# A four-layer graph network: block products with combined operands in layers 1 to 3, residual in HBM, projections by tile

## The reference, cut to what matters

```python
# N = 2708 nodes, 512 features, adj dense fp32 (2708 x 2708), all layers use the same adj
h = relu(layernorm(x)); x = x + relu(D(adj + I)D h @ W0)       # layer 0
h = relu(layernorm(x)); x = x + (D' adj D' h) @ W1.T + b1      # layer 1
h = relu(layernorm(x)); x = x + relu(D(adj + I)D h @ W2)       # layer 2
h = relu(layernorm(x))                                         # layer 3
x_b = adj @ (h @ Wg) + bg
e = where(adj != 0, exp(-leaky_relu(s_left[:, None] + s_right[None, :])), 0)
x_a = (e / (e.sum(1) + 1e-5)) @ (h @ Wsa)
x = x + sigmoid(gate_a * x_a + gate_b * x_b)
```

## Time and profile before

| | us |
|---|---|
| median of 3 runs | 1829.09 (1829.09 to 1830.65) |
| profiled execution | 1828.71 |
| its span, first to last instruction | 1826.9 |
| TensorE matmul busy | 1774.1 (97%) |
| VectorE busy | 900.4 (49%) |
| ScalarE busy | 693.5 (38%) |
| GpSimd busy | 273.5 (15%) |
| all DMA | 268.78 MB, mean 147 GB/s |

### The profile page before, as it was taken

How to read it: one execution, slowest core, us unless ns; L and a number is a source line. 1 busy time by engine, 2 the same in 40 slices (tenths; PEclk the granted TensorE clock), 3 DMA queues, 4 the chain that set the end, 5 groups by cost and what they waited for, 6 DMA issues and landing times.

```text
span 1826.9 us, 23918 instructions
## 1 busy us (share of the span) xinstructions
PE 1774.1 (97%) x9324; PEld 886.7 (49%) x9324; DVE 900.4 (49%) x1835; ACT 693.5 (38%) x1174; POOL 273.5 (15%) x222
## 2 busy tenths in 40 slices
PE   3999999999999999999999999999999999999996
PEld 1444446544444475444445654444466444444453
DVE  5776656656354445302032312544411577877765
ACT  5674444445333333101022212111000467768654
POOL 0001021112000000000000000311100355545431
PEclk9999999999999999999999999999999999999999
DMA  9974543575755568222431463332323333434422
GB/s 393 362 279 142 167 141 100 187 241 189 225 180 147 178 181 265 92 82 82 124 104 48 118 214 129 102 98 88 103 89 102 104 108 95 123 106 118 122 60 95
DMA packets 167425, 268.78 MB, mean 147 GB/s; under 512 B 17464, under 2 KB 78624, under 8 KB 164092
## 3 DMA queue, kind: packets, MB, share of 16 engines
q1 hardware_dynamic: 167312, 267.25, 46.4%
HBM read 208.79 MB, written 58.40 MB: 146 GB/s over the span
## 4 chain that ended last, share of the span: by engine, by line
PE 92%; ACT 3%; DVE 3%; DMA 2%; issue 0%; SPq 0%; POOL 0%; DVEq 0%; ACTq 0%
PE ps L872 25%; PE ps L873 25%; PE ps L874 25%; PE ps L824 16%; PE ps L866 1%; DMA T<-in_adj 1%; ACT T L1324 1%; DMA RG<-in_adjT 1%; DVE RG L1105 1%; ACT Q L1341 0%; ACT RG L1393 0%; PE ps L920 0%; DVE HB L1074 0%; PE ps L931 0%; ACT stage L1511 0%
## 5 line engine op out<-in xcount | busy, mean ns | idle before, releaser
L872 PE MATMUL ps<-RG,HB 128*128 128x512 f16 (+3 forms) x2368 | 836.6, 354 | 9.4 <-DVE RG L1129 3.3
L873 PE MATMUL ps<-RG,HB 128*128 128x512 f16 (+3 forms) x2368 | 836.2, 354 | 0.0
L874 PE MATMUL ps<-RG,HB 128*128 128x512 f16 (+3 forms) x2368 | 836.1, 354 | 0.0
L872 PEld LDWEIGHTS ps<-RG,HB 128*128 128x128 f16 x2368 | 232.0, 98 | 234.5 <-issue 7.5
L874 PEld LDWEIGHTS ps<-RG,HB 128*128 128x128 f16 x2368 | 231.9, 98 | 222.7 <-issue 1.9
L873 PEld LDWEIGHTS ps<-RG,HB 128*128 128x128 f16 x2368 | 231.9, 98 | 219.5 <-issue 1.9
L824 PE MATMUL ps<-W,OT 128*128 128x512 f16 (+1 forms) x1320 | 290.3, 379 | 3.5 <-DVE OT L1297 3.5
L1135 DVE SCALAR_TENSOR_TENSOR OT<-ps,OT 128x512 f16<-128x512 f32 (+2 forms) x96 | 53.5, 619 | 355.2 <-ACT OT L1441 355.2
L824 PEld LDWEIGHTS ps<-W,OT 128*128 128x128 f16 (+1 forms) x1320 | 128.2, 98 | 160.4 <-issue 4.4
L1581 POOL TENSOR_TENSOR T<-T 128x512 f32<-128x512 f32 (+2 forms) x126 | 172.9, 1372 | 180.9 <-DVE T L1119 180.3
L1105 DVE SCALAR_TENSOR_TENSOR RG<-RG,cS 128x512 f16<-128x512 f32 (+2 forms) x174 | 123.0, 720 | 136.0 <-ACT RG L1393 135.7
(11 more groups left out here) (187 smaller groups left out, 1103.6 us busy)
## 6 DMA issues: line engine op xcount, KB each, us to landing
RG<-in_adjT SPq DMA_DIRECT2D x225, 256.0 KB, 3.0
RG<-Ad SPq DMA_DIRECT2D x152, 256.0 KB, 2.6
Ad<-RG SPq DMA_DIRECT2D x84, 256.0 KB, 3.3
T<-in_adj SPq DMA_DIRECT2D x14, 1354.0 KB, 8.3
...
```

Source lines behind the costliest of these rows:

```text
L872: eng.matmul(o, h[0], hi, start=j == 0, stop=False)
L873: eng.matmul(o, h[0], lo, start=False, stop=False)
L874: last = eng.matmul(o, h[1], hi, start=False, stop=False)
```

## The change

In layers 1 to 3 the chunk's columns are cut in two halves and the features in two halves of 256. With row tiles j and j+1 as a pair, the chunk's sum over the pair is a 2x2 by 2x2 block product. It is computed with seven block products in place of eight, of combinations `T1..T4` of the adjacency blocks and `S1..S4` of the h blocks (the Strassen-Winograd form). Each of the seven products sums up in a bank of its own over ten pairs; tiles 20 and 21 are added directly as plain blocks. A matmul has half the chunk's width, 256, 128 or 202 columns. After the last pair and tile the seven sums are combined to the four output blocks (`gather`, `evacuate`); seven of eight banks are in use and the next chunk takes them over in the order of `SUMS`, the eighth (`x`) is for projections.

The combinations of the adjacency are made by GpSimd in fp32 (`sums`), then split. In layer 1 a unit (one pair, seven blocks, hi and lo) is kept in HBM, and layers 2 and 3 load units; in layer 2 the units on the diagonal are made again from raw tiles. The h combinations are made by GpSimd too (`h_sums`); there are seven slots in HB in place of four. SBUF for this comes from the residual: `xs` is gone, tiles are loaded (`x_load`) and kept (`x_keep`) in HBM through six buffers around each use. Projections are put tile by tile into the next chunk (`spaced`), for one bank. Weights for layers 1 to 3 are all split in layer 0 and loaded back.

```diff
+T2, A11, T4, A21, A22, T1, T3 = range(7)
+FIRST = ((H12, A21, "b"), (S4, A22, "d"), (S1, T1, "f"), (S3, T3, "g"))
+SECOND = ((S2, T2, "c"), (H11, A11, "a"), (H22, T4, "e"))
+SUMS = {GW: dict(a=3, b=4, c=2, d=5, e=0, f=6, g=7, x=1)}
+for _g in range(GW + 1, GE):
+    _o = SUMS[_g - 1]
+    SUMS[_g] = dict(b=_o["x"], d=_o["a"], f=_o["c"], g=_o["g"], c=_o["b"], a=_o["e"], e=_o["f"], x=_o["d"])
...
+def fly(g, j):
+    return g < 12 or g < 18 and (on_diagonal(g, j) or j < 20 and on_diagonal(g, j ^ 1)) or g >= GE
...
+    def spaced(u, g):
+        p, now = CHUNKS[g][0], g + 1
+        lead, gap = (8, 4) if now % 6 == 4 else (9, 4.5) if now % 6 in (0, 5) else (9, 9)
+        for i, t in enumerate(tiles(g)):
+            v = later(u, lead + gap * i)
+            plan(v, "project", g, t, SUMS[now]["x"])
+            if p < 3:
+                plan(max(u + 1, later(u, gap * i)), "x_load", "post", p, t)
+            post(max(v + 1, later(v, 1.5)), p, t)
...
     tensor, "agg" of layers 1 to 3
+                    if j < 20:
+                        for slot, k, to in FIRST if j % 2 == 0 else SECOND:
+                            pe.wait_ge(*h_ready(l, slot, J))
+                            if J == 0:
+                                opened(bank[to])
+                            hi, lo = operand(g, j, k)
+                            for a in range(2):
+                                o = ps[bank[to]][:, 256 * a:256 * a + n]
+                                h = [HB[:, slot, J, i, a * P:a * P + P] for i in range(2)]
+                                eng.matmul(o, h[0], hi, start=J == 0 and a == 0, stop=False)
+                                eng.matmul(o, h[0], lo, start=False, stop=False)
+                                last = eng.matmul(o, h[1], hi, start=False, stop=to in "acg" and J == 9 and a == 1)
+                    for to, o_h, o_a in (("b", 0, 0), ("d", D, n), ("e", 256, 0), ("f", 256, n)):   # tiles 20, 21
...
     gpsimd
+                elif kind == "sums":
+                    eng.tensor_tensor(unit[:, T1:T3 + 1, :], unit[:, T4:A22 + 1:2, :], unit[:, A11:T4 + 1, :],
+                                      ALU.subtract).then_inc(s_tsum, 1)
+                    pool.wait_ge(s_tsum, 3 * n - 2)
+                    eng.tensor_tensor(part[T2], part[A22], part[T1], ALU.subtract).then_inc(s_tsum, 1)
+                    pool.wait_ge(s_tsum, 3 * n - 1)
+                    eng.tensor_tensor(part[T4], part[A21], part[T2], ALU.subtract).then_inc(s_tsum, 1)
...
     scalar, vector: "gather" after tile 19, "evacuate" after tile 21
+                    eng.mul(block_of(0)[:, :, 0:half(g)], bank_halves(g, "a"), 2.0 ** -14).then_inc(s_ca, 1)
+                    eng.scalar_tensor_tensor(block_of(1)[:, :, 0:half(g)], bank_halves(g, "c"), 2.0 ** -14,
+                                             block_of(0)[:, :, 0:half(g)], ALU.mult, ALU.add).then_inc(s_cv, 1)
+                    eng.scalar_tensor_tensor(block_of(2)[:, :, 0:half(g)], bank_halves(g, "g"), 2.0 ** -14,
+                                             block_of(1)[:, :, 0:half(g)], ALU.mult, ALU.add).then_inc(s_cv, 1)
+                    for k, (to, src) in enumerate(((0, 0), (3, 2), (2, 2), (1, 1), (1, 1))):
+                        eng.scalar_tensor_tensor(block_of(to)[:, :, 0:h], bank_halves(g, "beffd"[k]), 2.0 ** -14,
+                                                 block_of(src)[:, :, 0:h], ALU.mult, ALU.add).then_inc(s_cs, 1)
+                    for k, (c, a, b) in enumerate(BLOCKS):
+                        eng.tensor_tensor(ot_block(g, 1, a, b), block_of(c)[:, :, 0:h], ot_block(g, 0, a, b),
+                                          ALU.subtract).then_inc(s_otlo, 1)
...
     sync
+                elif kind == "x_load":
+                    v = tuple(of)
+                    n, t = VISITS.index(v), of[2]
+                    if n >= NV:
+                        past = VISITS[n - NV]
+                        if past[0] == "fin":
+                            sync.wait_ge(s_mixo, s("mix_out", past[2], TILE[past[2]]))
+                        else:
+                            sync.wait_ge(*VKEPT[past])
...
+                        sync.wait_ge(*VKEPT[visit_before(v)])
+                        eng.dma_start(xt(*v), xd[t, 0:rows(t), :]).then_inc(VLOADED[v][0], 16)
```

More of the change, by code:

```diff
@@ L134, in cost, with free_of @@
+def free_of(*user):
+    return [stage for before in BEFORE[user] for stage in freed(before)]
 def cost(key):
-    return 2.6 * width(key[1]) / D
+    g, j = key[1:]
+    if not winograd(g):
+        return 2.6 * width(g) / D
+    return (24 if j < 20 and j % 2 == 0 else 18 if j < 20 else 24 if j == 20 else 8) * half(g) * 0.109 / 256
 CLOCK = [0.0]
@@ L168, in schedule @@
     plans = {}
-    fetched = split = scored = masked = quiet = 0
-    splits = [k for k in SEQ if k[1] < GP or k[1] >= GE]
+    fetched = split = summed = scored = masked = quiet = 0
+    splits = [k for k in SEQ if fly(*k[1:])]
+    units = [k for k in splits if winograd(k[1]) and k[2] < 20 and k[2] % 2 == 0]
     scores = [k for k in splits if k[1] >= GE]
@@ L177, in have, with near, last_tile @@
         return all(stage in s.no for stage in stages)
+    def near(key, u, steps, us):
+        return AT[key] <= (later(u, us) if winograd(key[1]) else u + steps)
+    def last_tile(g):
+        return max([f for f in range(g % 2, g, 2) if fly(f, NT - 1)], default=None)
     def ahead(u):
-        nonlocal fetched, split, scored, masked
+        nonlocal fetched, split, summed, scored, masked
         while scored < len(scores) and AT[scores[scored]] <= u + 6 and scored < masked + 2:
-            if not have(("row_out", scores[scored][1])):
+            if not have(("row_out", scores[scored][1]), *free_of("sc_a")):
                 break
@@ L190, in ahead @@
             masked += 1
-        while split < len(splits) and AT[splits[split]] <= u + LA:
+        while summed < len(units) and near(units[summed], u, 0, 14):
+            g, j = units[summed][1:]
+            if not have(("fetch", "agg", g, j), ("fetch", "agg", g, j + 1)):
+                break
+            put("sums", g, j)
+            summed += 1
+        while split < len(splits) and near(splits[split], u, LA, 9.6):
             g, j = splits[split][1:]
@@ L194, in ahead @@
                 break
-            if j < NT - 1 and not have(*freed(user_before("sp", g, j))):
+            if winograd(g):
+                if j < 20 and not have(("sums", g, whole(j))) or j < NT - 1 and not have(*free_of("un", g, whole(j))):
+                    break
+            elif j < NT - 1 and not have(*free_of("sp", g, j)):
                 break
```

925 lines of the change are left out of this document (559 added, 366 removed).

## The result

The changed kernel takes 1853.05 us (median of 4 runs, 1851.15 to 1854.17) against 1829.09 (4 runs beside it): ratio 1.0128, 95% interval 1.011 to 1.0145. It is **24 us slower**, where 1749 was forecast. The profiled execution took 1852.62 us with a span of 1850.8.

The account below looks back on a forecast made before the run. TensorE was taken as the bound, time being matmul count times pace: 1828.71 - 93 (matmuls) + 8 (layer 1) + 4 (turnover) + 1 (end) = 1748.7, with the median's 0.4 1749 us; range 1736 to 1792.

Parts of the forecast that it names:

- The sum on TensorE: Layers 1 to 3: matmul time falls from 292.9 to 261.7 us a layer, a gain of 93 us in three layers.
- Rival B: Narrow matmuls in layers 1 to 3 are bound by the 98 ns weight load: 72 us, total 1821; chance 0.03.
- The bias, factor and weight steps that move into layer 0 take the cover they have now: Layer 0: these moved steps stay hidden as before; no time was added for them.
- Layer 0 and the attention pass keep theirs too: Layer 0 and attention pass: their matmuls stay as they were, so no change in the TensorE sum.
- Layer 1, 8 us: Layer 1: DMA and GpSimd/VectorE interference together add 8 us; ends 0 and 60.
- Rival A: Layer 1 isn't bound by TensorE; whole-duration lock or late DMA costs 37 us in place of 8, total 1778; chance 0.18.
- Demand is 90 to 100%, not over it: Layer 1: GpSimd plus VectorE two-SBUF-input work, added as 333 us against TensorE's 319, overlaps a little and so about fits.
- DMA: Layer 1: 19 MB a wide chunk needs 55 to 63 us against 59.7; last chunk some 6 us late, partly covered.
- Turnover, 4 us: Chunk ends: handing seven sum banks over is hidden except before the narrow chunk and in layer 1; 4 us, bounds 0 and 97.
- rival C: Bank hand-over uncovered at each of 18 chunk ends, 5.4 us each: 97 us, total 1842, slower than before; chance 0.09.
- Residual in HBM, end: Residual tiles moving through six buffers cost 0 us; at the end the last add waits for one more load, 1 us.

Follow-up runs that it names:

- x_comb: Changed kernel with H sums on VectorE, longer split lookahead, earlier gates' bank read, later weights 2, plus three layer 1 cuts (two-column sums, shortened keeps and restores): 1775.0 us.

## Why the prediction was wrong, by its steps

- **The sum on TensorE** was right: 256, 202 and 128 columns start 0.109, 0.087 and 0.056 us apart, chunks 13 to 15 take 59.7 us without a stall, as the working said. Rival B is out. Only the layer in which two tiles' projections fall was missed: 5.2 us are in layer 1 and not in the attention pass, 0 in the sum.
- **"The bias, factor and weight steps that move into layer 0 take the cover they have now"**, with "Layer 0 and the attention pass keep theirs too": 0 us, measured +29.9 in layer 0. This is the step that failed first, and the prediction had no rival for it. The cover was there, but the sums of H are a new hop over GpSimd in a chain of in-order queues, and I priced GpSimd's 2.9 us, not who stands behind it nor what stands before. Without the changes of kind 15.2 us are gone, with the sums on VectorE 12.4, which overlap and don't add; with the sums on VectorE, lookahead and the later date 27.1 of 29.9.
- **Layer 1, 8 us**: 53. Rival A (37, at most 60) is what happened in size, and the port is one part of it. "Demand is 90 to 100%, not over it" counted VectorE's instructions with two SBUF inputs alone, by their busy time. The two-column tensor_scalar shows that others wait too, and up to a whole GpSimd instruction, however short they are. The Trainium skill says so ("SBUF — State Buffer", Who interferes with whom: copy, cast and tensor_scalar can, with operands that allow it, enter modes that take the shared pair), and I had used only the half on two inputs. And beside each other both engines take longer than the working had them: the sums of a unit 3.85 us for 2.7, its splits 2.76 for 2.3. It is no lock on all of both engines' work either: chunk 7 holds 39.6 us of GpSimd and 46.6 of VectorE in its 59.7, without a stall. Measured: GpSimd's sums 20.3, which holds the port and the sums' own time, keeps 4.1, restores 6.3 alone and 8.2 with the others, 9.4 more with layer 0's and VectorE's edits, 10.5 left.
- **DMA**: "from just hidden to 3 us late a chunk", with 6 us in the last, was near: 4 + 8 us. Chunk 7 moved 292 GB/s at DMA share 0.83 without a wait.
- **Turnover, 4 us; rival C**: right where the engines are on time (chunks 13 to 15 no wait at the start, 16 and 17 0.6 and 0.3 us). In layer 1 VectorE is late and it adds up to 11 us of waits, at chunk 12 it costs most of 9.8, and in layer 3 a second reader of the handed-over bank, the gates, cost 13, and the attention pass waits 5.6 us at its start: I had listed the bank's readers without the order of VectorE's queue between them.
- **Residual in HBM, end**: 0 and 1 us; no run separates the first from the DMA term. The attention pass with the tail came out 1.2 us longer, with 5.8 us of matmuls less.
- Missing altogether was the clock: the half-pace matmuls behind stalls, some 31 us of the 104 and part of the terms above. No row that the prediction used shows it; the trace of before has it in its start, where 512-column matmuls behind a wait start 0.43 us apart from 25.3 to 30.8 us.

The sum: 29.9 + 50.4 + 11.3 + 16.7 us of misses in layers 0 to 3, less the 5 us taken for turnover and end, plus 1.2 in the attention pass, give 104 us, which is 1853 - 1749. Of the 50.4, 5.2 are the projections that the attention pass has less.

What stays open: how the 20.3 us divide between the port and the length of the sums, since a layer 1 with true sums made elsewhere was not tried; the cause of the last 10.5 us of layer 1, of which TensorE's waits in x_comb hold 7.7, all for VectorE (3.4 for bank additions, 2.7 for residual additions, 1.4 for tile 20 of h); and whether chunk 6's wait for tile 20 is VectorE's load alone. No kernel that computes everything brought layer 1 under 373.7 us.
